# Turning three sets of normalised rows by transposing transfers instead of on the matrix engine, with new order lists

## Chip, cores and metric

The kernel runs on one core of one Trainium2 chip, as one program. The metric is device time in microseconds (us), lower is better. The engines are PE (TensorE, with its weight loads PEld), DVE (VectorE), ACT (ScalarE), POOL (GpSimd) and SP (SyncE, which issues every transfer of this kernel).

## What is computed

The input is `x` of shape (2, 4096, 512) in f32. Two blocks follow each other, each with a residual:

```python
x = x + time_mix(layernorm(x))      # k = x@Wk.T, r = v = x@Wr.T, RWKV recurrence, sigmoid(r)*y, @Wo
x = x + ffn(layernorm(x))
def ffn(x):
    h = rmsnorm(x, gamma1)
    q = h @ Wq + bq;  kv = (h @ Wdown + bdown) @ Wup + bup      # latent of 64
    x = x + (softmax_over_heads(q k / sqrt(32)) v) @ Wo + bo    # 16 heads attend to each other per token
    h2 = rmsnorm(x, gamma2)
    gate = softmax(h2 @ Wg + bg)
    return x + einsum('btd,edf,bte->btf', h2, We, gate)         # 8 experts, all dense
```

Every large product is done in three f16 passes: an operand is split into a high and a low half (`x_hi`, `x_lo`), and hi·hi, lo·hi and hi·lo are summed (`PASSES`). So a product needs its activations as two f16 halves with channels on the partitions, while normalisation needs tokens on the partitions. The step between them is a turn, three times per tile: `mix_turn` (input of the time mix), `att_turn` (input of attention) and `fin_turn2` (input of gate and experts).

## The kernel before

The tokens are cut into `NT` = 32 tiles of 256 tokens, two subtiles (`SUB`) of 128, alternating between the two batch rows. Each engine runs a program of its own through `pipeline` (L561): a head list, then a list `X_ORDER` repeated for `i` = 4 to 30, then a tail list. An entry ("moe", 7, 4) means: step `moe` with part 7 for tile i − 4. So the order on every engine is fixed by hand-written lists, several tiles are in flight, and an engine that waits holds up all that stands behind it in its list. The engines meet through semaphores: `Steps` counts them, `done(t, step, k)` gives the value to wait for.

Per tile the steps that matter here are:

- `pre_load` (SP, L636) brings `xk`, `pre_stats` and `pre_norm` make the layernorm rows, `mix_turn` turns them, `mix_k` and `mix_v` (48 matmuls of 256 columns each) project. DVE then scans the recurrence in two halves (`mix_decay`, `mix_sum`, `mix_value`, `mix_scan`, `mix_rec`, `mix_gate`, `mix_split`), and `mix_project` (24 matmuls) multiplies by Wo.
- `att_norm`, `att_turn`, `att_latent`, `att_q`, `att_up` make q, k and v. SP restacks q and k with 24 transfers (`att_up`, L646). `att_max` 0 to 3 computes 8 banks of scores whose row maxima DVE reduces (L1234), `att_m` turns the maxima, which SP sends back as two extra rows of `qs`, `att_scores` and `att_probs` 0 to 7 follow. DVE's `att_vlo` (L1229) makes the low half of v.
- `fin_back`, `fin_project` give `x2`, `fin_square` and `fin_norm2` its rows, `fin_turn2` turns them into `h2t`, `fin_gate` is the gate's product, `moe_gate` its softmax on DVE, and `moe` 0 to 15 are 8 experts times 2 subtiles, 12 matmuls of 512 columns each (L1333), each added to `acc` by DVE (L1311). PE's `moe` u waits for DVE's `moe` u − 2, as there are two banks. `moe_store` (L667) stores `acc`. There is one `h2t`, so its writer waits for the last `moe` of the tile before.

A turn before the change is 8 matmuls against the identity (`turn`, L1349) into two PSUM banks, then per bank one ACT instruction for the high half and one DVE instruction for the low half (`lo`):

```python
ins = nc.tensor.transpose(banks[b][:, c * T + s * P:c * T + (s + 1) * P],
                          rows_[:, s, (2 * b + c) * P:(2 * b + c + 1) * P], ident[:, :])
...
act.wait_ge(*fin_pe.done(t, "T2", b))
nc.scalar.activation(h2t[:, 0, 2 * b:2 * b + 2, :], mix_bank[b][:, :], ACT.Copy, scale=XS)
...
lo(h2t[:, 1, 2 * b:2 * b + 2, :], mix_bank[b][:, :], XS, h2t[:, 0, 2 * b:2 * b + 2, :])
```

The banks are shared: 0 and 1 for the experts, 2 and 3 for the time mix, both output projections, the turns and the gate, 4 to 7 a ring for attention (`ATT_USES`).

## Time and profile before

| | |
|---|---|
| median of 3 runs | 2760.3 us (2759.11 to 2760.59) |
| profiled execution, its own time | 2758.6 us |
| its span | 2756.5 us |
| mean granted PE clock | 0.975 |
| busy share of the span: PE, DVE, ACT, POOL | 94%, 77%, 56%, 34% |
| transfers | 119.29 MB, all but the instructions' own on one queue, issued by SP |

The span goes from the first to the last instruction, and the execution's own time is 2.1 us longer. A busy share is a mean over start-up, steady part and end. A granted clock of 1.00 is 2.4 GHz, 0.50 is 1.2 GHz. In a timeline an entry merges neighbouring instructions of one line, and its length reaches beyond the start of the next entry, since the ends of matmuls are modelled and pipelined; so durations below are taken from start to start.

### The profile page before, as it was taken

How to read it: one execution, taken by the hardware profiler on the slowest of the kernel's cores; microseconds unless marked ns; L12 is line 12 of the kernel's file. 1: busy time of each engine (PE TensorE's matmuls, PEld its weight loads, DVE VectorE, ACT ScalarE, POOL GpSimd, SP SyncE). 2: the span in 40 equal slices, each digit the busy share in tenths (PEclk: the TensorE clock that was granted, in tenths of full speed). 3: DMA queues.
4: the chain of work that ended last, by engine and by line, in shares of the span. 5: the costliest groups of instructions: out<-in, count | busy, mean ns of one | idle time of the engine just before them, and what ended most of it. 6: DMA issues, size and time to landing. Idle time of an engine off the chain costs nothing.

```text
span 2756.5 us, 48625 instructions
## 1 busy us (share of the span) xinstructions
PE 2586.4 (94%) x18896; PEld 1580.4 (57%) x18896; DVE 2133.6 (77%) x3647; ACT 1531.3 (56%) x2799; POOL 948.9 (34%) x970
## 2 busy tenths in 40 slices
...
DMA packets 845322, 119.29 MB, mean 43 GB/s; under 512 B 813587, under 2 KB 813715, under 8 KB 845075
## 3 DMA queue, kind: packets, MB, share of 16 engines
...
## 4 chain that ended last, share of the span: by engine, by line
PE 88%; DVE 4%; ACT 4%; POOL 2%; SPq 1%; issue 1%; DMA 0%; ACTq 0%; DVEq 0%; POOLq 0%
PE bank L1333 78%; PE bank L1355 3%; PE bank L1500 2%; PE bank L1471 2%; PE bank L1511 2%; DVE h2t L1104 1%; PE bank L1487 1%; POOL w_e L693 1%; ACT h2t L939 1%; PE bank L1512 1%; ACT ot L789 1%; DVE mcol L1234 0%; ACT t L888 0%; POOL pr L734 0%; DVE acc L1311 0%
## 5 line engine op out<-in xcount | busy, mean ns | idle before, releaser
L1333 PE MATMUL bank<-w_e,h2t 128*128 128x512 f16 x6144 | 1383.4, 380 | 2.8 <-DVE acc L1311 2.0
L1333 PEld LDWEIGHTS bank<-w_e,h2t 128*128 128x128 f16 x6144 | 592.1, 98 | 665.9 <-issue 4.4
L1311 DVE SCALAR_TENSOR_TENSOR acc<-bank,gates,acc 128x512 f32<-128x512 f32 x512 | 371.9, 736 | 120.4 <-PE bank L1333 117.4
L906 ACT ACTIVATE pr<-bank,plog,col 128x512 f32<-128x512 f32 x256 | 198.7, 776 | 407.9 <-PE bank L1500 405.5
L734 POOL TENSOR_TENSOR pr<-pr 128x512 f16<-128x512 f32 x256 | 295.7, 1160 | 182.3 <-ACT pr L908 180.9
L721 POOL TENSOR_TENSOR qo<-t,qo 128x256 f16<-128x256 f32 x128 | 106.5, 832 | 493.4 <-ACT qo L891 490.3
L1142 DVE TENSOR_TENSOR_SCAN wkv<-e,wkv 128x256 f32<-128x256 f32 x256 | 210.8, 864 | 74.6 <-ACT e L834 73.4
L1166 DVE RECIPROCAL zz<-zz 128x256 f32<-128x256 f32 x128 | 218.9, 1732 | 29.4 <-POOL zz L703 29.3
L1333 PE MATMUL bank<-w_o,xo 128*128 128x512 f16 x768 | 176.2, 387 | 46.9 <-DVE xo L1104 46.9
L908 ACT ACTIVATE pr<-bank,plog,col 128x512 f16<-128x512 f32 x256 | 197.8, 773 | 0.0
L1333 PE MATMUL bank<-xo,w_k 128*128 128x256 f16 x1536 | 172.9, 273 | 2.4 <-DVE xo L1104 2.4
L1333 PE MATMUL bank<-xo,w_r 128*128 128x256 f16 x1536 | 172.9, 273 | 0.5 <-ACT xk L814 0.5
L1333 PE MATMUL bank<-ht,w_q 128*128 128x256 f16 x1536 | 173.2, 273 | 0.0
L1333 PE MATMUL bank<-w_o,oo 128*128 128x512 f16 x768 | 171.0, 379 | 1.0 <-DVE oo L1104 1.0
L750 POOL TENSOR_TENSOR acc<-x,x 128x512 f32<-128x512 f32 x64 | 80.3, 1276 | 261.5 <-DMA result<-acc 261.5
L1333 PEld LDWEIGHTS bank<-xo,w_k 128*128 128x128 f16 x1536 | 150.0, 98 | 26.0 <-DVE xo L1104 2.7
L1234 DVE TENSOR_REDUCE mcol<-bank 128x4 f32<-128x512 f32 x256 | 158.3, 681 | 3.6 <-PE bank L1487 3.6
L1249 DVE TENSOR_REDUCE on<-bank 128x132 f32<-128x264 f32 x256 | 103.3, 424 | 74.3 <-PE bank L1512 74.3
L1333 PEld LDWEIGHTS bank<-ht,w_q 128*128 128x128 f16 x1536 | 150.5, 98 | 17.5
L1333 PEld LDWEIGHTS bank<-xo,w_r 128*128 128x128 f16 x1536 | 150.2, 98 | 17.8 <-issue 0.8
L1333 PEld LDWEIGHTS bank<-w_o,xo 128*128 128x128 f16 x768 | 75.0, 99 | 134.2 <-DVE xo L1104 47.2
L703 POOL TENSOR_TENSOR zz<-wkv,zz 128x512 f32<-128x512 f32 x64 | 94.1, 1470 | 158.4 <-DVE ev L1153 158.3
...
## 6 DMA issues: line engine op xcount, KB each, us to landing
qs<-qo SPq DMA_DIRECT2D x384, 64.0 KB, 2.4
ks<-k SPq DMA_DIRECT2D x384, 64.0 KB, 2.4
...
ks<-in_attn_Wr SPq DMA_DIRECT2D x1, 1024.0 KB, 10.0
```

The source lines that it names most:

```text
L703: nc.gpsimd.tensor_tensor(zz[:, :, :], wkv[:, 2, :, 0:T], zz[:, :, :], ALU.add).then_inc(mix_pool.sem, 1)
L721: nc.gpsimd.tensor_tensor(grouped(dst, 1)[:, :, b, :], t32[:, b % 2, :].rearrange("p (g j) -> p g j", g=G), grouped(dst, 0)[:, :, b, :], A ...
L734: nc.gpsimd.tensor_tensor(pr16[:, 1, k % 2, :], pr[:, k % 2, :], pr16[:, 0, k % 2, :], ALU.subtract).then_inc(att_pool.sem, 1)
L906: nc.scalar.activation(pr[:, k % 2, :], att_bank[ATT_BANK["S", k]][:, :], ACT.Exp, bias=plog[:, 0:1], scale=colof["soft"])\
L908: nc.scalar.activation(pr16[:, 0, k % 2, :], att_bank[ATT_BANK["S", k]][:, :], ACT.Exp, bias=plog[:, 0:1], scale=colof["soft"])\
L1142: V.tensor_tensor_scan(wkv[:, n, c, 1:T + 1], e1[:, c, :], src[:, c, :], wkv[:, n, c, 0:1], ALU.mult, ALU.add).then_inc(mix_dve.sem, 1)
L1166: V.reciprocal(zz[:, c, :], zz[:, c, :]).then_inc(mix_dve.sem, 1)
L1234: V.tensor_reduce(mcol[:, 4 * k:4 * k + 4], att_bank[ATT_BANK["M", k]][:, :].rearrange("p (g x) -> p g x", g=4), AX, ALU.max).then_inc(att ...
L1249: V.tensor_reduce(on[:, 4 * k:4 * k + 4, :], pv.rearrange("p g (l d) -> p g d l", l=2), AX, ALU.add).then_inc(att_dve.sem, 1)
L1311: V.scalar_tensor_tensor(out=acc[:, s, :], in0=moe_bank[u % 2][:, :], scalar=gates[:, s, e:e + 1], in1=acc[:, s, :], op0=ALU.mult, op1=ALU ...
L1333: ins = nc.tensor.matmul(dst, left(a), right(b), start=(n == 0), stop=(n == last))
L1355: ins = nc.tensor.transpose(banks[b][:, c * T + s * P:c * T + (s + 1) * P], rows_[:, s, (2 * b + c) * P:(2 * b + c + 1) * P], ident[:, :])
```

## The change

The 8 matmuls of each turn go. ACT and DVE now split the rows before they are turned, token by token (two instructions each per turn, as before, now from SBUF to SBUF): high and low halves of 128 x 512 f16 values per subtile, into buffers laid over others (`row16` over `v32`, `hr16` over `k16`, `on16` over `on`). SP then issues four transposing transfers per turn, each of 128 KB, of which each waits for its half of its subtile; they land in `xo16`, `ht16` and `h2t`. PE waits for all four. The writer of `h2t` is now SP, which waits for the last `moe` of the tile before. New waits keep the laid-over buffers apart. The turns' PSUM uses are gone, and the attention ring has two uses fewer. The order lists of all five engines are written anew. The diff, cut (heads, tails and the lists of ACT and POOL are left out but for a few lines; `att_turn` and `fin_turn2` on ACT and DVE change as `mix_turn` does):

```diff
-ATT_USES = ([("T", 0), ("T", 1), ("D", 0), ("Q", 0), ("Q", 1), ("K", 0), ("K", 1), ("V", 0), ("V", 1),
+ATT_USES = ([("D", 0), ("Q", 0), ("Q", 1), ("K", 0), ("K", 1), ("V", 0), ("V", 1),
...
 PE_ORDER = [
...
-    ("att_probs", 6, 3), ("att_probs", 7, 3), ("mix_turn", 0, 1), ("moe", 9, 4), ("mix_k", 0, 1), ("att_turn", 0, 2),
-    ("mix_v", 0, 1), ("att_latent", 0, 2), ("att_q", 0, 2), ("moe", 10, 4), ("att_up", 0, 2), ("moe", 11, 4),
-    ("moe", 12, 4), ("fin_project", 0, 3), ("moe", 13, 4), ("moe", 14, 4), ("moe", 15, 4), ("fin_turn2", 0, 3),
-    ("att_max", 0, 2), ("att_max", 1, 2), ("fin_gate", 0, 3), ("moe", 0, 3), ("att_max", 2, 2), ("att_max", 3, 2),
...
+    ("moe", 8, 4), ("att_probs", 6, 3), ("att_probs", 7, 3), ("moe", 9, 4), ("moe", 10, 4), ("mix_k", 0, 1),
+    ("mix_v", 0, 1), ("att_latent", 0, 2), ("att_q", 0, 2), ("moe", 11, 4), ("att_up", 0, 2), ("fin_project", 0, 3),
+    ("moe", 12, 4), ("moe", 13, 4), ("moe", 14, 4), ("moe", 15, 4), ("att_max", 0, 2), ("att_max", 1, 2),
+    ("att_max", 2, 2), ("att_max", 3, 2), ("moe", 0, 3), ("att_m", 0, 2), ("fin_gate", 0, 3), ("moe", 1, 3),
+    ("moe", 2, 3), ("att_scores", 0, 2), ("att_scores", 1, 2), ("moe", 3, 3), ("moe", 4, 3), ("att_probs", 0, 2),
...
 DVE_HEAD = [
...
-    ("att_max", 0, 0), ("att_max", 1, 0), ("att_max", 2, 0), ("mix_split", 0, 1), ("mix_decay", 1, 1),
-    ("mix_sum", 1, 1), ("att_max", 3, 0), ("att_m", 0, 0), ("mix_value", 1, 1), ("mix_scan", 1, 1), ("mix_rec", 2, 1),
...
+    ("att_max", 2, 0), ("att_max", 3, 0), ("att_m", 0, 0), ("mix_sum", 1, 1), ("mix_value", 1, 1), ("mix_scan", 1, 1),
...
 DVE_ORDER = [
...
-    ("att_vlo", 0, 2), ("fin_project", 0, 3), ("moe", 13, 4), ("mix_decay", 1, 1), ("moe", 14, 4), ("moe", 15, 4),
-    ("fin_turn2", 0, 3), ("att_max", 0, 2),
...
+    ("mix_rec", 1, 1), ("fin_project", 0, 3), ("mix_gate", 0, 1), ("att_vt", 0, 2), ("moe", 12, 4),
+    ("mix_split", 0, 1), ("moe", 13, 4), ("fin_turn2", 0, 3), ("mix_decay", 1, 1), ("moe", 14, 4), ("moe", 15, 4),
+    ("att_vlo", 0, 2), ("att_max", 0, 2), ("att_max", 1, 2), ("att_max", 2, 2), ("mix_sum", 1, 1), ("att_max", 3, 2),
+    ("att_m", 0, 2), ("moe_gate", 0, 3),
...
 SP_HEAD = [
     ("pre_load", 0, 0), ("set_ident", 0, -1), ("set_load", 0, -1), ("set_load", 1, -1), ("set_load", 2, -1),
-    ("set_load", 3, -1), ("set_load", 4, -1), ("set_experts", 0, -1), ("set_experts", 1, -1), ("mix_k", 0, 0),
-    ("set_experts", 2, -1), ("set_experts", 3, -1), ("set_experts", 4, -1), ("set_experts", 5, -1),
-    ("pre_load", 0, 1), ("set_experts", 6, -1), ("set_experts", 7, -1), ("set_masks", 0, -1), ("mix_k", 0, 1),
-    ("att_up", 0, 0), ("att_m", 0, 0), ("pre_load", 0, 2), ("att_up", 0, 1), ("pre_load", 0, 3),
+    ("set_load", 3, -1), ("set_load", 4, -1), ("mix_turn", 0, 0), ("mix_k", 0, 0), ("set_experts", 0, -1),
+    ("set_experts", 1, -1), ("set_experts", 2, -1), ("set_experts", 3, -1), ("set_experts", 4, -1),
+    ("set_experts", 5, -1), ("set_experts", 6, -1), ("set_experts", 7, -1), ("set_masks", 0, -1), ("pre_load", 0, 1),
+    ("mix_turn", 0, 1), ("mix_k", 0, 1), ("att_turn", 0, 0), ("att_up", 0, 0), ("att_m", 0, 0), ("pre_load", 0, 2),
+    ("mix_turn", 0, 2), ("att_turn", 0, 1), ("att_up", 0, 1), ("fin_turn2", 0, 0), ("att_m", 0, 1),
+    ("pre_load", 0, 3), ("mix_k", 0, 2), ("mix_turn", 0, 3), ("att_turn", 0, 2),
 ]
 
 SP_ORDER = [
-    ("mix_k", 0, 2), ("att_m", 0, 3), ("att_up", 0, 2), ("pre_load", 0, 0), ("moe_store", 0, 4),
+    ("att_up", 0, 2), ("fin_turn2", 0, 3), ("moe_store", 0, 4), ("pre_load", 0, 0), ("att_m", 0, 2), ("mix_k", 0, 1),
+    ("mix_turn", 0, 0), ("att_turn", 0, 1),
 ]
 
...
+        row16 = v32[:, :, :].rearrange("p b t -> p (b t)").bitcast(F16).rearrange("p (l s c) -> p l s c", l=2, s=SUB)
...
+        on16 = on[:, :, :].rearrange("p g d -> p (g d)")[:, 0:SUB * C].bitcast(F16).rearrange("p (l s c) -> p l s c", l=2, s=SUB)
...
+        hr16 = k16[:, :, :, :].rearrange("p l b t -> p l (b t)").rearrange("p l (s c) -> p l s c", s=SUB)
...
+        turn_in = Steps(sem("turn_in"), 16, x=4)
+        turn2_in = Steps(sem("turn2_in"), 16, h=4)
+        turn1_in = Steps(sem("turn1_in"), 16, h=4)
...
+            def mix_turn(t, _):
+                if t.back(1):
+                    sp.wait_ge(*mix_pe.done(t.back(1), "O"))
+                for s in range(SUB):
+                    for l, (steps, step) in enumerate(((mix_act, "x_hi"), (mix_dve, "x_lo"))):
+                        sp.wait_ge(*steps.done(t, step, s))
+                        sp.dma_start(xo16[:, l, :, s * P:(s + 1) * P], row16[:, l, s, :], transpose=True).then_inc(turn_in.sem, 16)
...
+            def att_turn(t, _):
+                if t.back(1):
+                    sp.wait_ge(*att_dve.done(t.back(1), "vt"))
+                for s in range(SUB):
+                    for l, (steps, step) in enumerate(((att_act, "h_hi"), (att_dve, "h_lo"))):
+                        sp.wait_ge(*steps.done(t, step, s))
+                        sp.dma_start(ht16[:, l, :, s * P:(s + 1) * P], hr16[:, l, s, :], transpose=True).then_inc(turn1_in.sem, 16)
...
+            def fin_turn2(t, _):
+                if t.back(1):
+                    sp.wait_ge(*moe_pe.done(t.back(1), "u"))
+                else:
+                    sp.wait_ge(elo_done, E * CB)
+                for s in range(SUB):
+                    for l, (steps, step) in enumerate(((fin_act, "h2_hi"), (fin_dve, "h2_lo"))):
+                        sp.wait_ge(*steps.done(t, step, s))
+                        sp.dma_start(h2t[:, l, :, s * P:(s + 1) * P], on16[:, l, s, :], transpose=True).then_inc(turn2_in.sem, 16)
...
             def mix_turn(t, _):
-                for b in range(2):
-                    act.wait_ge(*mix_pe.done(t, "T", b))
-                    if b == 0 and t.back(1):
-                        act.wait_ge(*mix_pe.done(t.back(1), "O"))
-                    nc.scalar.activation(xo16[:, 0, 2 * b:2 * b + 2, :], mix_bank[b][:, :], ACT.Copy, scale=XS)\
-                        .then_inc(mix_act.sem, 1)
+                if t.back(1):
+                    act.wait_ge(*mix_dve.done(t.back(1), "e2v_1"))
+                for s in range(SUB):
+                    act.wait_ge(*pre_act.done(t, "norm", s))
+                    nc.scalar.activation(row16[:, 0, s, :], xk_rows[:, s, :], ACT.Copy, scale=XS).then_inc(mix_act.sem, 1)
...
             def mix_turn(t, _):
-                for b in range(2):
-                    dve.wait_ge(*mix_act.done(t, "x_hi", b))
-                    lo(xo16[:, 1, 2 * b:2 * b + 2, :], mix_bank[b][:, :], XS, xo16[:, 0, 2 * b:2 * b + 2, :]).then_inc(mix_dve.sem, 1)
+                for s in range(SUB):
+                    dve.wait_ge(*mix_act.done(t, "x_hi", s))
+                    lo(row16[:, 1, s, :], xk_rows[:, s, :], XS, row16[:, 0, s, :]).then_inc(mix_dve.sem, 1)
 
...
+                if k == 0 and t.back(1):
+                    dve.wait_ge(*turn2_in.done(t.back(1), "h"))
...
 
-                if use == "T":
+                if use == "K":
                     if t.back(1):
                         pe.wait_ge(*mix_dve.done(t.back(1), "x1", k))
-                elif use == "K":
-                    pe.wait_ge(*mix_dve.done(t, "x_lo", k))
                 elif use == "V":
                     pe.wait_ge(*mix_act.done(t, "k", k))
...
 
-            def mix_turn(t, _):
-                if not t.back(1):
-                    pe.wait_ge(ident_in, 16)
-                pe.wait_ge(*pre_act.done(t, "norm"))
-                turn(xk_rows, mix_bank, mix_pe, mix_pe.sem, lambda b: mix_free(t, "T", b))
-
...
-                pe.wait_ge(*mix_dve.done(t, "x_lo"))
+                pe.wait_ge(*turn_in.done(t, "x"))
...
 
             pipeline(pe, PE_HEAD, PE_ORDER, PE_TAIL,
-                     {f"set_{name}": lambda _, k, name=name: set_turn(name, k) for name in TURNED} | {"mix_turn": mix_turn, "mix_k": mix_k, "mix_v": mix_v, "mix_project": mix_project,
-                          "att_turn": att_turn, "att_latent": att_latent, "att_q": att_q, "att_up": att_up, "att_max": att_max, "att_m": att_m, "att_scores": att_scores, "att_probs": att_probs,
...
```

## Rows read from the trace of the kernel before

**Rows 1.** The page: busy time by engine, with shares of the span.

```profile
PE 2586.4 (94%) x18896; PEld 1580.4 (57%) x18896; DVE 2133.6 (77%) x3647; ACT 1531.3 (56%) x2799; POOL 948.9 (34%) x970
```

**Rows 2.** Busy time by stretch in the steady part (span, PE, PEld, DVE, ACT, POOL, PEclk, DMA).

```profile
1000.00:1500.00 500.00, 495.26 (x3667) 306.21 (x3666) 404.77 (x680) 284.91 (x518) 175.94 (x181) 1.00 0.23 40
```

**Rows 3.** PE over one tile's period (start us, us, line, tile, count, idle before).

```profile
1200.72 5.34 PE L1333 MATMUL bank<-w_e,h2t 128*128 128x512 f16 x24
...
1230.52 1.22 PE L1355 MATMUL bank<-ident,xk 128*128 128x128 f32 x8
1231.57 2.75 PE L1333 MATMUL bank<-w_e,h2t 128*128 128x512 f16 x12
...
1274.53 1.04 PE L1355 MATMUL bank<-ident,ot 128*128 128x128 f32 x8
1275.40 1.06 PE L1487 MATMUL bank<-ks,qs 104*128 104x128 f16 x16
1277.20 0.76 PE L1333 MATMUL bank<-w_g,h2t 128*128 128x8 f16 x24 [0.74 <-DVE h2t L1104]
1277.82 2.75 PE L1333 MATMUL bank<-w_e,h2t 128*128 128x512 f16 x12
1280.41 1.06 PE L1487 MATMUL bank<-ks,qs 104*128 104x128 f16 x16
1281.30 5.34 PE L1333 MATMUL bank<-w_e,h2t 128*128 128x512 f16 x24
```

**Rows 4.** DVE over the same period.

```profile
1265.87 1.22 DVE L1229 TENSOR_TENSOR vp<-hrow,vp 128x1024 f16<-128x1024 f32 x1
...
1274.80 0.75 DVE L1311 SCALAR_TENSOR_TENSOR acc<-bank,gates,acc 128x512 f32<-128x512 f32 x1 [0.82 <-PE bank L1333]
...
1277.06 2.48 DVE L1234 TENSOR_REDUCE mcol<-bank 128x4 f32<-128x512 f32 x4
...
1279.45 0.23 DVE L1285 SCALAR_TENSOR_TENSOR gl<-bank,col,bg_row 128x16 f32<-128x16 f32 x1
...
1282.15 0.75 DVE L1311 SCALAR_TENSOR_TENSOR acc<-bank,gates,acc 128x512 f32<-128x512 f32 x1
...
1285.86 1.39 DVE L1142 TENSOR_TENSOR_SCAN wkv<-e,wkv 128x256 f32<-128x256 f32 x2
```

**Rows 5.** SP's queue over the same period: issues of transfers.

```profile
1254.57 5.64 SPq L655 DMA_DIRECT2D qs<-qo  x8
...
1269.05 2.81 SPq L659 DMA_DIRECT2D ks<-k  x4
```

**Rows 6.** The page: DMA packets, and issues with size and time to landing.

```profile
DMA packets 845322, 119.29 MB, mean 43 GB/s; under 512 B 813587, under 2 KB 813715, under 8 KB 845075
...
qs<-qo SPq DMA_DIRECT2D x384, 64.0 KB, 2.4
```

**Rows 7.** PE busy time and granted clock (PEclk) around one idle stretch late in the run.

```profile
2490.00:2491.00 1.00, 0.00 (x0) 0.88 0.76 91
2491.00:2497.00 6.00, 5.53 (x60) 0.50 0.69 182
2497.00:2498.00 1.00, 1.00 (x5) 0.70 0.00 0
```

**Rows 8.** PE around the same idle stretch.

```profile
2491.47 0.81 PE L1333 MATMUL bank<-w_g,h2t 128*128 128x8 f16 x24 [3.40 <-DVE h2t L1104]
...
2495.70 3.69 PE L1333 MATMUL bank<-w_e,h2t 128*128 128x512 f16 x12
```

**Rows 9.** PE in the start-up.

```profile
23.60 5.40 PE L1333 MATMUL bank<-xo,w_k 128*128 128x256 f16 x48
...
81.79 8.30 PE L1333 MATMUL bank<-w_o,xo 128*128 128x512 f16 x24 [46.88 <-DVE xo L1104]
...
155.64 0.40 PE L1493 MATMUL bank<-ident,mcol 128*32 128x128 f32 x1 [11.22 <-DVE mcol L1234]
```

**Rows 10.** SP's queue in the start-up.

```profile
32.03 0.91 SPq L626 DMA_DIRECT2D bg_row<-in_ffn_bg  x2
```

More of the change, by code:

```diff
@@ L146 @@
-    ("att_probs", 2, 0), ("att_scores", 4, 0), ("att_probs", 3, 0), ("att_scores", 5, 0), ("att_probs", 4, 0),
-    ("att_scores", 6, 0), ("att_probs", 5, 0), ("att_scores", 7, 0), ("mix_project", 0, 1), ("mix_turn", 0, 2),
-    ("att_probs", 6, 0), ("att_probs", 7, 0), ("mix_k", 0, 2), ("att_turn", 0, 1), ("mix_v", 0, 2),
-    ("att_latent", 0, 1), ("att_q", 0, 1), ("fin_project", 0, 0), ("att_up", 0, 1), ("fin_turn2", 0, 0),
-    ("fin_gate", 0, 0), ("att_max", 0, 1), ("att_max", 1, 1), ("att_max", 2, 1), ("moe", 0, 0), ("att_max", 3, 1),
@@ L154 @@
+    ("att_latent", 0, 1), ("att_q", 0, 1), ("fin_project", 0, 0), ("att_up", 0, 1), ("att_max", 0, 1),
+    ("att_max", 1, 1), ("att_max", 2, 1), ("att_max", 3, 1), ("moe", 0, 0), ("att_m", 0, 1), ("fin_gate", 0, 0),
+    ("moe", 1, 0), ("moe", 2, 0), ("att_scores", 0, 1), ("att_scores", 1, 1), ("moe", 3, 0), ("moe", 4, 0),
+    ("att_probs", 0, 1),
 ]
 PE_ORDER = [
-    ("att_scores", 4, 3), ("moe", 7, 4), ("att_probs", 3, 3), ("att_scores", 5, 3), ("moe", 8, 4),
-    ("att_probs", 4, 3), ("att_scores", 6, 3), ("att_probs", 5, 3), ("att_scores", 7, 3), ("mix_project", 0, 2),
@@ L170 @@
-    ("att_probs", 4, 4), ("att_scores", 6, 4), ("att_probs", 5, 4), ("att_scores", 7, 4), ("mix_project", 0, 3),
-    ("moe", 9, 5), ("mix_turn", 0, 2), ("att_probs", 6, 4), ("att_probs", 7, 4), ("moe", 10, 5), ("mix_k", 0, 2),
-    ("mix_v", 0, 2), ("att_turn", 0, 3), ("fin_project", 0, 4), ("att_latent", 0, 3), ("att_q", 0, 3),
-    ("att_up", 0, 3), ("moe", 11, 5), ("moe", 12, 5), ("moe", 13, 5), ("fin_turn2", 0, 4), ("moe", 14, 5),
-    ("moe", 15, 5), ("fin_gate", 0, 4), ("att_max", 0, 3), ("att_max", 1, 3), ("att_max", 2, 3), ("att_max", 3, 3),
@@ L180 @@
-    ("att_probs", 7, 3), ("mix_k", 0, 1), ("mix_v", 0, 1), ("att_turn", 0, 2), ("moe", 10, 4), ("moe", 11, 4),
-    ("att_latent", 0, 2), ("att_q", 0, 2), ("att_up", 0, 2), ("fin_project", 0, 3), ("moe", 12, 4), ("moe", 13, 4),
-    ("moe", 14, 4), ("moe", 15, 4), ("fin_turn2", 0, 3), ("fin_gate", 0, 3), ("att_max", 0, 2), ("att_max", 1, 2),
-    ("att_max", 2, 2), ("att_max", 3, 2), ("moe", 0, 3), ("att_m", 0, 2), ("moe", 1, 3), ("moe", 2, 3),
-    ("att_scores", 0, 2), ("att_scores", 1, 2), ("moe", 3, 3), ("att_probs", 0, 2), ("att_scores", 2, 2),
```

412 lines of the change are left out of this document (206 added, 206 removed), and 3 rows, old and new, of the table POOL_HEAD.

## The prediction

> **What bounds the kernel now.** I read the page's busy times first: PE is busy for 94% of the span, DVE for 77% [rows 1]. A share over the whole run hides the stages, so I went on to stretches: in the steady part PE is busy for 495.3 of 500 us at full clock, DVE for 404.8 [rows 2]. So PE's own work sets the pace there, and what it stops doing is worth its full length, if nothing else becomes late. PE's timeline gives the period of a tile: the same pair of expert steps starts at 1200.72 and 1281.30, 80.58 us apart [rows 3].
>
> **What the change takes from PE.** The time mix's turn takes 1231.57 - 1230.52 = 1.05 us, the experts' turn 1275.40 - 1274.53 = 0.87 [rows 3]; attention's stands between them in form and count and I take 0.87 too. That is 2.79 us per tile, 89 us in 32 tiles. PE also waits 0.74 us per tile for the halves of `h2t` before the gate [rows 3]. If nothing else moved, 3.5 us per tile would go: over the 29 tiles of the sum below 102 us, or 2657. ACT and DVE keep two instructions each per turn, of the same size and count, now from SBUF. I cost that at nothing: both have idle time in a period, DVE 19% of it [rows 2]. The PSUM uses that go free banks that nobody was seen to wait for.
>
> **What it puts in their place.** I follow each turn in the new lists.
>
> *Experts.* This is the place that decides. There is one `h2t`, so SP may begin its four transfers only when `moe` 15 of the tile before is done, and `moe` 0 needs all four. Between them PE now has only `att_max` 0 to 3; then come `moe` 0, `att_m`, `fin_gate`, `moe` 1, `moe` 2. Call the end of `moe` 15 time 0. Before, `moe` 2 started at 1281.30 + 2.59 - 1274.53 = 9.4 (a `moe` step is 1280.41 - 1277.82 = 2.59) [rows 3]. The rest of the period is 80.6 - 9.4 = 71.2; without the two other turns, and with `att_m` (0.1) moved into the stretch, it becomes 69.2. The new period is 69.2 plus the new start of `moe` 2.
>
> Even with free transfers DVE's list sets a floor for it. DVE reads `moe` 15 from 0.27 for 0.67 us, then does `att_vlo` (1.14 of its 1.22, as neighbours overlap by 0.08), six reductions of 0.60, `mix_sum` (1.3) and two more reductions: 8.2 us [rows 4]. Before, `att_vlo` was long done and `mix_sum` came later; now both lie ahead of `att_m`, which on PE lies ahead of the gate. After `att_m` the gate's product takes 0.6 [rows 3], and from the first instruction of `moe_gate` to the end of `moe` 0 on DVE are 1282.15 + 0.67 - 1279.45 = 3.4 us [rows 4], for which `moe` 2 waits: 8.2 + 0.1 + 0.6 + 0.2 + 3.4 = 12.5. The period would be 81.7, **1.1 us longer than now**, although PE has 2.8 us less to do.
>
> Now the transfers. No row shows a transposing one. The nearest is SP's restacking: a 64 KB transfer occupies SP's queue for 5.64 / 8 = 0.70 us [rows 5] and lands 2.4 us after its issue began [rows 6], 1.7 after its end. With 384 for q and as many for k, and 813,587 packets under 512 B, a transfer is some 1,060 pieces of 64 bytes [rows 6]. A turn's transfer has twice the bytes. I take twice the time, **1.4 us each**, on the guess that the cost goes with the pieces; the ends are 0.70 (it costs what the row shows) and 2.8 (its pieces are half as long). The last of four lands at 0.1 + 5.6 + 1.7 = 7.4 (4.6 at the low end, 13.0 at the high). `moe` 0 then runs from 7.4 to 10.0, `att_m` and gate end at 10.7, and 0.2 + 3.4 later `moe` 2 starts, at 14.2: +2.8 us per tile. At the low end the floor of 12.5 stands; a landing up to 5.6 costs nothing.
>
> The Trainium skill (Advanced Engine Details and Errata, DMA Advanced Topics, on the X-bar transpose) says that transposing transfers run as fast as plain ones. By that the sum would end at its low end, near 2783.
>
> *The clock.* Between 0 and 7.4 PE has 1.8 us of work. Late in the run PE stood idle for 3.4 us before a gate [rows 8]; by the shares of two rows its clock fell to 0.50, which is 1.2 GHz, at 2490.8 and came back at 2497.6 [rows 7], and the `moe` step in between is listed with 3.69 us [rows 8] instead of 2.75 [rows 3]. The new stretch holds over 5 us of idleness in 7.4, so I expect this in every tile: of some 6.8 us at half clock about 4 fall on `moe` 0 and the gate's product, and half of those are lost: +2.0. Per tile **+4.8 us**.
>
> *Time mix.* From the end of `mix_project` to `mix_k` PE has three `moe` steps and four short ones, about 8.6 us. DVE still has the second update of `x1` and the first low half to make, 0.7 each, the size of its `moe` steps [rows 4]; three transfers follow: 1.5 + 4.2 + 1.7 = 7.4. Hidden, and exposed from some 1.8 us per transfer on. *Attention.* It has the two projections more as cover: 96 matmuls of 256 columns, the columns of four `moe` steps, 10.4 us. Hidden as well.
>
> *SP.* Twelve transfers more are 16.8 us of its queue per tile, beside 24 x 0.70 = 16.9 for restacking and a few loads, within 80. `fin_turn2` stands behind `att_up`, whose last issue ended at 1269.05 + 2.81 = 1271.86 [rows 5]. PE's way from `att_q` to `att_max` becomes one `moe` step and one turn shorter, 3.46 us, so on that tile's scale `moe` 15 would end at 1275.40 - 3.46 = 1271.94: SP is free just then, and the last of `ks` lands 1.6 us later, which the floor hides. Behind `fin_turn2` wait `moe_store`, `pre_load` and `att_m`'s two transfers; the last is needed after 11, SP is free at 7.
>
> *Start-up.* SP reaches the first turn only after the constants, at 33 us [rows 10]; with 5.6 + 1.7 `mix_k` starts at 40, not at 23.6 [rows 9]. But PE then waited 46.9 us for `mix_project` [rows 9] on DVE and ACT work for weights that the new lists put later; I make it 2 us later in all. Against that, `att_m` waited 11.2 us because `mix_sum` stood ahead of it on DVE [rows 9], and no longer does. Net -8 (+15 to -25).
>
> *Sum.* 27 periods and two more in head and tail: 29 x 4.8 = +139, -8. The profiled execution took 2758.6 us (1.7 below the median of 2760.3): **2890 us**.
>
> **Rivals.**
>
> - *Cheap transfers, or the clock holds.* Landing below 5.6, or no fall: +1.1 to +2.8 per tile, 2783 to 2832. For it: the restacking rows. Against: the idleness.
> - *Dearer transfers.* At 2.8 us each `moe` 0 starts at 13.0, and with more of it at half clock `moe` 2 at 22.3: +10.9 per tile, 3067. Should a piece be 8 bytes (5.6 us each), `moe` 0 starts at 24 and the time mix's turn shows by 15 us as well: +38 per tile, about 3850. The Trainium skill (VectorE: DVE Perf Modes, the three transpose paths) gives 1309 ns for one 128x128 block by transposing DMA; four blocks in a row would be 5.2 us, and with that this worst case. DMA is only 23% busy [rows 2], which speaks against it.
> - *Faster.* The turns pay in full, 29 x 3.5: 2657. Place: between `moe` 15 and `moe` 2. It needs `moe` 2 to start by 11.4, where the 2.8 us saved balance; DVE's list gives 12.5 at the least, so it needs reductions or the gate's softmax 1.1 us shorter and transfers landed by 4.5.
> - *No change*: the low end, with a start-up some 25 us shorter.
>
> **Chances.** Forecast 0.50 (2835 to 2960), cheap 0.20, dearer 0.15, worst 0.04, faster 0.07, no change 0.04. A measurement here can tell about 0.2%, 5.5 us. The range, 2783 to 3060, spans the two ends of a transfer's price.
>
> **What would show it.** In the new profile: L1355 gone from PE; between `moe` 15 and `moe` 0 an idle stretch ended by a transfer into `h2t`, about 5 us per tile; granted clock below 1.00 once per tile; a period near 85.4; transposing issues of 1.4 us on SP; `mix_k` and `att_latent` without waits. I am wrong if `moe` 2 starts within 11 us of `moe` 15's end, or if the period is below 80.6.

## The result, and the profile after

The changed kernel takes 2887.94 us (median of 3 runs, 2886.72 to 2896.34) against 2760.3, a ratio of 1.0475 with a 95% interval of 1.0459 to 1.0491. It is slower, as forecast (2890, range 2783 to 3060). The profiled execution took 2896.3 us with a span of 2894.2, so it stands 8.4 us above the median; the one of before stood 1.7 below its own.

The page of after, busy times [rows 1] and the chain that ended last:

```profile
PE 2607.8 (90%) x18128; PEld 1529.4 (53%) x18128; DVE 2096.8 (72%) x3647; ACT 1527.1 (53%) x2799; POOL 963.8 (33%) x970
...
PE 66%; SPq 14%; ACT 8%; DVE 4%; DMA 3%; POOL 3%; issue 2%; ACTq 0%; DVEq 0%; POOLq 0%
```

The chain of before:

```profile
PE 88%; DVE 4%; ACT 4%; POOL 2%; SPq 1%; issue 1%; DMA 0%; ACTq 0%; DVEq 0%; POOLq 0%
```

PE has 768 instructions less (24 per tile, the turns) and is busy *longer*. What it no longer does is made up elsewhere: the expert products, unchanged in number, are listed with 1443.5 us instead of 1383.4, mostly because of `moe` 0 at half clock (below), and those of `att_max` with 103.7 instead of 73.9. SP's queue now holds 14% of the chain, where it held 1%.

The last wait of each stage is seen best in PE's waits by what ended them, for the stretch 500 to 2500 us (some 24 tiles; us in total, times, longest):

```profile
PE bank L1501 <- DMA ks<-k: 47.8, 23, 3.3
PE bank L1361 <- DMA h2t<-on: 29.6, 23, 2.9
PE bank L1501 <- DVE mcol L1261: 10.1, 39, 0.7
```

Before, the only one of note was that for the halves of `h2t`:

```profile
PE bank L1333 <- DVE h2t L1104: 21.2, 25, 3.4
```

In the changed kernel there is none for the time mix's or attention's transfers. Where does the time go within a tile? PE's timeline between `moe` 15 and `moe` 2, first in one of the 3 of 27 steady tiles in which `moe` 0 ran at full clock [rows 3 has the stretch of before]:

```profile
1255.80 3.67 PE L1501 MATMUL bank<-ks,qs 104*128 104x128 f16 x32 [2.19 <-DMA ks<-k]
1260.55 2.76 PE L1361 MATMUL bank<-w_e,h2t 128*128 128x512 f16 x12 [1.08 <-DMA h2t<-on]
1263.15 0.27 PE L1507 MATMUL bank<-ident,mcol 128*32 128x128 f32 x1
...
1263.87 2.75 PE L1361 MATMUL bank<-w_e,h2t 128*128 128x512 f16 x12
1267.09 2.76 PE L1361 MATMUL bank<-w_e,h2t 128*128 128x512 f16 x12 [0.47 <-DVE acc L1339]
```

and one tile on, as in most:

```profile
1338.63 1.58 PE L1501 MATMUL bank<-ks,qs 104*128 104x128 f16 x20 [2.18 <-DMA ks<-k]
...
1343.33 5.12 PE L1361 MATMUL bank<-w_e,h2t 128*128 128x512 f16 x12 [1.11 <-DMA h2t<-on]
1348.28 0.27 PE L1507 MATMUL bank<-ident,mcol 128*32 128x128 f32 x1
...
1349.00 5.56 PE L1361 MATMUL bank<-w_e,h2t 128*128 128x512 f16 x24
```

`moe` 15 ends at 1255.80 - 2.19 = 1253.61 and 1338.63 - 2.18 = 1336.45, and `moe` 0 starts 6.9 us later in both. In the first, `moe` 2 starts 13.5 us after `moe` 15's end, in the second 1349.00 + 2.6 - 1336.45 = 15.2; before it was 9.4. The rest of the period is 82.84 - 13.5 = 69.4 us. The second tile's `moe` 0 takes 5.1 us instead of 2.8, with the same shape, count and operands. The granted clock (third column from the end) shows why, and shows that it fell in the first tile too, only earlier:

```profile
1256.00:1259.00 3.00, 3.00 (x30) 2.63 (x28) 2.68 (x5) 0.29 (x1) 0.00 (x0) 0.50 0.40 88
1343.00:1348.00 5.00, 4.67 (x12) 1.64 (x13) 2.23 (x4) 0.00 (x0) 2.48 (x2) 0.50 0.62 210
```

In the first tile PE ran at 0.50 during `att_max` and was back at full clock before `moe` 0. It lost next to nothing by that: `att_max` took 3.67 us, and in the second tile, where the clock fell only behind 1341, 1341.61 + 0.61 - 1338.63 = 3.6, with waits for DVE's reductions in between. The two other tiles with a fast `moe` 0 show the same (0.50 from 1680 to 1682 and from 2103 to 2105 us). So the clock falls in every steady tile, and in 24 of 27 the fall lies on `moe` 0. SP's queue and DVE in the second tile [rows 5, rows 4]:

```profile
1290.71 5.20 SPq L654 DMA_TRANSPOSE xo<-v  x4
1300.61 5.12 SPq L667 DMA_TRANSPOSE ht<-k  x4
1318.93 5.65 SPq L678 DMA_DIRECT2D qs<-qo  x8
...
1333.98 2.82 SPq L682 DMA_DIRECT2D ks<-k  x4
1336.90 5.23 SPq L698 DMA_TRANSPOSE h2t<-on  x4
```

```profile
1339.07 3.68 DVE L1261 TENSOR_REDUCE mcol<-bank 128x4 f32<-128x512 f32 x6 [0.33 <-PE bank L1501]
1342.66 1.38 DVE L1170 TENSOR_TENSOR_SCAN wkv<-e,wkv 128x256 f32<-128x256 f32 x2
1343.97 1.26 DVE L1261 TENSOR_REDUCE mcol<-bank 128x4 f32<-128x512 f32 x2
1348.60 0.28 DVE L1267 TENSOR_SCALAR m<-bank 32x128 f16<-32x128 f32 x1 [3.37 <-PE bank L1507]
```

A transposing transfer holds SP for 1.3 us, and the last of four lands 1343.33 - 1342.13 = 1.2 us after its issue ended. SP is busy with hardly a gap from 1318.93 to 1342.13: restacking, then the experts' turn. DVE is done with the maxima at 1345.2 and then waits 3.4 us for `att_m`, which stands behind the slow `moe` 0 on PE. DVE isn't the bound here.

A tile's period is read from the start of `att_m`'s one matmul, one row for 32 tiles; here of after, then of before (ns min/median/max, first and last start):

```profile
L1507 PE MATMUL bank<-ident,mcol x32: 272/273/421, 154.0 to 2789.5; 128*32 128x128 f32 x32
```

```profile
L1493 PE MATMUL bank<-ident,mcol x32: 272/273/396, 155.6 to 2663.3; 128*32 128x128 f32 x32
```

From tile 2 to tile 25 the mean period is 84.71 us after and 80.61 before: **+4.10**. Of the 137.7 us between the two spans, 94.3 lie in these 23 periods, 12.7 in the start-up (`att_m` of tile 2 at 331.7 instead of 318.9) and 30.6 in the last six tiles and the end. The profile of after stands 8.4 us above its median, some 0.3 us per tile, so its periods are a little long against the medians.

### The profile page after: what moved, and what is told of

Its sections match the earlier page's. It is cut to its first block, busy times and chain, and to the rows that moved or that the text cites. A ratio compares the mean times of both kernels' runs of the same rounds, so it can differ in the third digit from the quotient of the medians.

```text
span 2894.2 us, 47472 instructions
## 1 busy us (share of the span) xinstructions
PE 2607.8 (90%) x18128; PEld 1529.4 (53%) x18128; DVE 2096.8 (72%) x3647; ACT 1527.1 (53%) x2799; POOL 963.8 (33%) x970
## 4 chain that ended last, share of the span: by engine, by line
PE 66%; SPq 14%; ACT 8%; DVE 4%; DMA 3%; POOL 3%; issue 2%; ACTq 0%; DVEq 0%; POOLq 0%
PE bank L1361 61%; SPq L678 5%; SPq L698 4%; SPq L682 4%; DMA h2t<-on 3%; PE bank L1514 2%; ACT t L921 2%; PE bank L1525 1%; ACT qo L924 1%; PE bank L1485 1%; ACT e L862 1%; ACT e L858 1%; POOL w_e L726 1%; PE bank L1526 1%; DVE acc L1339 1%
## 5 line engine op out<-in xcount | busy, mean ns | idle before, releaser
L1361 PE MATMUL bank<-w_e,h2t 128*128 128x512 f16 x6144 | 1443.5, 392 | 51.5 <-DMA h2t<-on 45.5
L1361 PEld LDWEIGHTS bank<-w_e,h2t 128*128 128x128 f16 x6144 | 600.3, 100 | 777.9 <-issue 77.4
L767 POOL TENSOR_TENSOR pr<-pr 128x512 f16<-128x512 f32 x256 | 317.2, 1244 | 298.9 <-ACT pr L941 276.2
L1170 DVE TENSOR_TENSOR_SCAN wkv<-e,wkv 128x256 f32<-128x256 f32 x256 | 236.0, 963 | 103.7 <-ACT e L866 102.4
L1194 DVE RECIPROCAL zz<-zz 128x256 f32<-128x256 f32 x128 | 219.1, 1733 | 13.5 <-POOL zz L736 13.5
L1501 PE MATMUL bank<-ks,qs 104*128 104x128 f16 x1024 | 103.7, 262 | 111.7 <-DMA ks<-k 93.0
L1361 PE MATMUL bank<-xo,w_k 128*128 128x256 f16 x1536 | 179.2, 278 | 25.5 <-DMA xo<-v 25.5
L972 ACT ACTIVATE gl<-gl 128x16 f32<-128x16 f32 x32 | 6.9, 215 | 339.9 <-DVE gl L1319 339.9
```

What stands on the lines that cost most here:

```text
L767: nc.gpsimd.tensor_tensor(pr16[:, 1, k % 2, :], pr[:, k % 2, :], pr16[:, 0, k % 2, :], ALU.subtract).then_inc(att_pool.sem, 1)
L1170: V.tensor_tensor_scan(wkv[:, n, c, 1:T + 1], e1[:, c, :], src[:, c, :], wkv[:, n, c, 0:1], ALU.mult, ALU.add).then_inc(mix_dve.sem, 1)
L1194: V.reciprocal(zz[:, c, :], zz[:, c, :]).then_inc(mix_dve.sem, 1)
L1361: ins = nc.tensor.matmul(dst, left(a), right(b), start=(n == 0), stop=(n == last))
```

## Experiments

Three theories were set against each other. *Landing*: the loss sits between `moe` 15 and `moe` 2, since SP may write `h2t` only after `moe` 15. *Clock*: half of it is PE's clock falling in that gap. The rivals: SP's full queue (late `ks`), DVE's list, or the two hidden turns. All ratios below are to the kernel before, run on the same chip.

### The clock: spare products in the gap

```diff
+            def spare(t, count):
+                pe.wait_ge(*fin_dve.done(t, "x2", 1))
+                for _ in range(count):
+                    nc.tensor.matmul(mix_bank[1][:, :], w16["e0"][:, 0, 0, 0:P], w16["e0"][:, 0, 0, :], start=True, stop=True)
```

called with 8 ahead of `att_max` 0 and with 4 ahead of `moe` 0.

> The changed kernel with spare products in PE's two gaps (results thrown away): 8 matmuls of 512 columns between moe 15 and att_max 0, 4 between att_max 3 and moe 0, 0.22 us each, so 1.7 and 0.9 us inside gaps of 2.2 and 1.1 us. Clock theory: moe 0 runs for 5.0 us where the granted clock is 0.50 and 2.6 us where it is 1.00; kept busy, PE keeps its clock, the period goes from 84.7 to 82.6 us and the run from 2888 to about 2825. Rival, the clock falls for another reason or the loss is only the transfers': 2888, or a little more.

Measured: 2854.5 us, ratio 1.0348 (1.0333 to 1.0364), period 83.20. Busy times and granted clock (third column from the end) over 500 to 2500 us, then PE in one tile:

```profile
500.00:2500.00 2000.00, 1941.52 (x13873) 1139.38 (x13872) 1545.13 (x2646) 1089.61 (x1973) 696.47 (x700) 1.00 0.32 58
```

```profile
1399.18 1.89 PE L1496 MATMUL bank<-w_e 128*128 128x512 f16 x8
...
1406.33 2.76 PE L1361 MATMUL bank<-w_e,h2t 128*128 128x512 f16 x12 [1.00 <-DMA h2t<-on]
...
1412.90 2.76 PE L1361 MATMUL bank<-w_e,h2t 128*128 128x512 f16 x12 [0.50 <-DVE acc L1339]
```

In the changed kernel the clock of the same window was 0.96, and 24 of 27 tiles lost 2.2 us each at `moe` 0. With PE kept busy `moe` 0 runs at full clock in nearly every tile, though it still waits for its rows. That is worth 33 us by the medians, and 1.5 of the 4.1 us per tile by the profiles; the other 2.6 stay. I had expected 2.1 per tile and 2825 us. Part of what is missing is that PE now waits for DVE at `moe` 2, here 0.5 us and 10.4 us in all between 500 and 2500.

### SP's queue: four restacking transfers less

```diff
                         for n in first:
+                            if name == "k" and n == 2 and t.back(1):
+                                continue
```

> The changed kernel without 4 of the 24 restacking transfers of each tile but the first (rows 64 to 95 of ks keep the first tile's values, so attention's scores are others). SP is then free 2.8 us earlier and ks lands 2.8 us earlier. Landing theory (h2t's transfers can't start before moe 15 is done, whatever SP does): only the 0.4 us between moe 15's end and SP's first issue goes, and the 2.2 us wait of att_max turns into a longer wait of moe 0: 2888 - 31 x 0.4 = about 2875. Rival, SP's queue or DVE's reductions after the late ks set the end: 2.2 to 2.8 us less per tile, 2801 to 2820.

Measured: 2878.8 us, ratio 1.0434 (1.0418 to 1.0449): 9 us less than the changed kernel, period 84.17. In one tile of it:

```profile
1414.15 5.14 SPq L701 DMA_TRANSPOSE h2t<-on  x4
```

```profile
1413.95 1.06 PE L1504 MATMUL bank<-ks,qs 104*128 104x128 f16 x16
1417.05 0.40 PE L1504 MATMUL bank<-ks,qs 104*128 104x128 f16 x4 [2.04 <-DVE mcol L1264]
...
1420.49 5.15 PE L1364 MATMUL bank<-w_e,h2t 128*128 128x512 f16 x12 [1.03 <-DMA h2t<-on]
```

`att_max` starts at once, its wait goes elsewhere in the stretch, and `moe` 0 still starts 1420.49 - 1413.95 = 6.5 us after `moe` 15. So the largest wait in the list of waits, 47.8 us for `ks`, is worth 9: what ends the stretch is the landing of `h2t`. The theory that SP's late `ks` sets the pace, worth 2.2 to 2.8 us per tile, falls.

### The price of the landing: half the transfers, and twice as many

```diff
                         sp.wait_ge(*steps.done(t, step, s))
+                        if l == 1 and t.back(1):
+                            continue
                         sp.dma_start(h2t[:, l, :, s * P:(s + 1) * P], on16[:, l, s, :], transpose=True).then_inc(turn2_in.sem, 16)
```

> The changed kernel with only the two high halves of the experts' rows turned (the low halves in h2t keep the first tile's values). SP's part falls from 5.2 to 2.6 us. Landing theory: moe 0 no longer waits for a transfer and starts when att_max 3 is done, 1.1 us earlier: 2888 - 31 x 1.1 = 2854 if the clock falls as before, 2790 if it holds in every tile. Rival, DVE's list (att_vlo, reductions, mix_sum) holds att_m and with it moe 2: no gain beyond 0.5 us per tile, 2872 or more.

```diff
                         sp.dma_start(h2t[:, l, :, s * P:(s + 1) * P], on16[:, l, s, :], transpose=True).then_inc(turn2_in.sem, 16)
+                for n in range(2 * SUB):
+                    sp.dma_start(ot[:, :].bitcast(F16).rearrange("p (n b t) -> p n b t", n=4, b=CB)[:, n, :, :], on16[:, n % 2, n // 2, :], transpose=True).then_inc(turn2_in.sem, 16)
```

> The changed kernel with four more transposing transfers behind the experts' own four (same rows, into a buffer that is free then); moe 0 and the gate wait for all eight. Landing theory: SP's part grows from 5.2 to 10.4 us, moe 0 starts 5.2 us later and runs at half clock in every tile: +5.2 to +6 us per tile, 3050 to 3075. Rival, the price of a transfer is mostly the fixed wait for its landing, or DVE's list holds the stretch: +2.6 us per tile or less, under 2970.

Measured: half 2844.5 us, 1.0309 (1.0294 to 1.0324), period 82.91, -1.8; twice 3051.5 us, 1.1061 (1.1045 to 1.1078), period 89.71, +5.0. Four more transfers cost their 5.2 us of SP in full, as the landing theory has it; two fewer give back less than 2.6 (1.8, with the clock still falling), so that another bound shows below. PE's wait in the second kernel:

```profile
PE bank L1363 <- DMA ot<-on: 150.9, 23, 7.8
```

### The bound below: DVE's list

In `h2_half` PE waited for the maxima at `att_m` in 11 tiles. To keep the clock out of it, a pair was run with the 8 spare products, without and with this change of DVE's list:

```diff
-("moe", 14, 4), ("moe", 15, 4), ("att_vlo", 0, 2), ("att_max", 0, 2), ("att_max", 1, 2), ("att_max", 2, 2), ("mix_sum", 1, 1), ("att_max", 3, 2),
+("att_vlo", 0, 2), ("moe", 14, 4), ("moe", 15, 4), ("att_max", 0, 2), ("att_max", 1, 2), ("att_max", 2, 2), ("att_max", 3, 2),
...
-("moe", 0, 4), ("moe", 1, 4), ("mix_value", 1, 2),
+("moe", 0, 4), ("moe", 1, 4), ("mix_sum", 1, 2), ("mix_value", 1, 2),
```

> h2_half (only the high halves of the experts' rows turned) with 8 spare products in PE's wait between moe 15 and att_max 0, so that the clock holds. Floor theory: att_m waits for DVE's list (att_vlo, reductions, mix_sum), which ends 7.6 us after att_max began whatever the clock; moe 2 starts 13.1 us after moe 15 as in h2_half, the period is that of the tiles of h2_half in which the clock held, 82.3 us, and the run 2820 to 2844. Rival (DVE is no bound, only the clock): the period falls below 81.5 us, under 2805.

> h2_half_fill with DVE's list changed as in h2_half_dve (att_vlo ahead of moe 14, mix_sum's second half behind moe 1). Floor theory: with the clock held, att_m no longer waits for DVE and moe 2 starts 1.2 us earlier, 31 x 1.2 = 37 us less than h2_half_fill, less 1.0 us per tile if att_probs waits for POOL as in h2_half_dve: a difference of -6 to -37 us. Rival: as slow against h2_half_fill as h2_half_dve was against h2_half, +24 us; then the moved steps cost more elsewhere than DVE's list costs there.

Measured: 2854.5 (1.0345, 1.0329 to 1.0360) and 2836.3 us (1.0284, 1.0267 to 1.0301), periods 83.43 and 82.50. The first, by PE, DVE and POOL:

```profile
1410.82 2.76 PE L1364 MATMUL bank<-w_e,h2t 128*128 128x512 f16 x12
1415.22 0.28 PE L1517 MATMUL bank<-ident,mcol 128*32 128x128 f32 x1 [1.65 <-DVE mcol L1264]
...
1415.95 7.03 PE L1364 MATMUL bank<-w_e,h2t 128*128 128x512 f16 x24
```

```profile
1411.64 2.35 DVE L1173 TENSOR_TENSOR_SCAN wkv<-e,wkv 128x256 f32<-128x256 f32 x2
```

```profile
1411.81 3.23 POOL L786 TENSOR_TENSOR acc<-x,x 128x512 f32<-128x512 f32 x2 [14.00 <-DMA result<-acc]
```

Here the floor of the prediction is seen: PE stands 1.65 us for DVE's maxima, and the clock, kept at `moe` 0, falls one step later (`moe` 1 and 2 take 7.03 us, not 5.56). Such a 7.03 us pair stands in 8 of the steady tiles, and in others `moe` 0 is slow all the same. So the first run missed both of its forecasts: the 8 spare products, which should have kept the clock, made `h2_half` 10 us slower. The mean granted clock was 0.957, against 0.951 without them.

Moving the two DVE steps away is worth 18 us, within what was expected. PE's waits in the second run, 500 to 2500 us:

```profile
PE bank L1534 <- POOL pr L769: 23.4, 49, 0.7
PE bank L1510 <- DVE mcol L1263: 15.8, 76, 0.3
PE bank L1510 <- DMA ks<-k: 13.4, 17, 1.6
```

With half the transfers, a clock that mostly holds and DVE's list eased, the period is still 82.50, 1.9 us above that of before. What is left are these waits, of which that for POOL came with the moved steps, and the 1.7 us of spare products. So half of the landing, the clock and DVE's list together give back 2.2 of the 4.1 us, and what the rest would take isn't isolated.

The same change of DVE's list without spare products made the kernel slower:

> h2_half (only the high halves of the experts' rows turned, the low ones in h2t keep the first tile's values) with DVE's list changed: att_vlo ahead of moe 14, and mix_sum's second half behind moe 1 instead of between the reductions. Floor theory: in h2_half att_m waits for DVE, whose list between moe 15 and att_m is 2.5 us longer than it need be; without that moe 2 starts 1.5 us earlier, 2844 - 31 x 1.5 = 2798. Rival, DVE is no bound there: 2844 unchanged, or slower for what the moved steps now hold up.

Measured: 2868.2 us (1.0381, 1.0358 to 1.0403), 24 more than `h2_half`. The period grew by 1.2 us, from 82.91 to 84.08. The list of PE's waits has one that `h2_half` didn't have, 1.0 us per tile:

```profile
PE bank L1527 <- POOL pr L769: 23.0, 48, 0.5
```

And `moe` 0 took 5.2 us in one tile, at 1419.48, and 3.9 in the corresponding one of `h2_half`; the mean clock was 0.944 against 0.951. How the 24 us divide between POOL and the clock is not shown.

### The time mix's turn: how well is it hidden?

The same addition to `mix_turn`, from `row16` into the dead `xk`.

> The changed kernel with four more transposing transfers behind the time mix's own four (into the rows' old buffer); mix_k waits for all eight. In the changed kernel the last one lands 2.3 us before mix_k starts. So 5.2 us more should show as 2.9 us per tile: 2888 + 31 x 2.9 = 2978. With the slack of the prediction, 1.2 us, it would be +4.0, 3012. Rival, a wait at mix_k only takes the place of the waits for ks and h2t later in the tile (SP's queue gains the same time): less than 1 us per tile, under 2920.

Measured: 3047.7 us, 1.1043 (1.1026 to 1.1059), period 89.19, +4.5. PE's waits, and `mix_k` itself:

```profile
PE bank L1363 <- DMA xk<-v: 70.5, 22, 3.8
```

```profile
1372.76 7.08 PE L1363 MATMUL bank<-xo,w_k 128*128 128x256 f16 x48 [3.70 <-DMA xk<-v]
```

The wait is 3.2 us per tile, so 5.2 us more leave 2.0 hidden: the slack, nearly as the profile of after had it. But in most tiles part of `mix_k` then also runs at half clock, and it is listed with 7.08 us, not the 5.4 of the changed kernel. I had left that out, and 2978 was too low by 70. A wait of some 3 us on PE costs 4.5 to 5.

### Is the experts' turn alone to blame?

The obvious repair leaves the experts' turn on PE (code of before) and the two others to transfers. It was tried with three sets of steady lists, DVE's following PE's. PE's, first:

```diff
-("moe", 15, 4), ("att_max", 0, 2), ("att_max", 1, 2), ("att_max", 2, 2), ("att_max", 3, 2), ("moe", 0, 3), ("att_m", 0, 2), ("fin_gate", 0, 3), ("moe", 1, 3), ("moe", 2, 3), ("att_scores", 0, 2), ("att_scores", 1, 2), ("moe", 3, 3), ("moe", 4, 3), ("att_probs", 0, 2),
+("moe", 15, 4), ("fin_turn2", 0, 3), ("att_max", 0, 2), ("att_max", 1, 2), ("fin_gate", 0, 3), ("moe", 0, 3), ("att_max", 2, 2), ("att_max", 3, 2), ("moe", 1, 3), ("moe", 2, 3), ("att_m", 0, 2), ("moe", 3, 3), ("moe", 4, 3), ("att_scores", 0, 2), ("att_scores", 1, 2), ("moe", 5, 3), ("att_probs", 0, 2),
```

> The turn of the time mix and that of attention by transfers as in the changed kernel, the experts' turn on PE as before, with the order between moe 15 and moe 3 as before. Landing theory (all of the loss sits at h2t, the two other turns are hidden): PE keeps 1.9 us less to do than before, the period is 78.7 to 79.5 us, the run 2700 to 2730, faster than both. Rival, the two hidden turns cost too (their transfers, or the longer chain through SP's queue): a period of 80.6 us or more, 2760 and above.

The second, from `att_scores` 5 to `moe` 11:

```diff
+("att_scores", 5, 3), ("mix_project", 0, 2), ("att_probs", 4, 3), ("att_scores", 6, 3), ("att_probs", 5, 3), ("att_scores", 7, 3), ("moe", 8, 4), ("att_probs", 6, 3), ("att_probs", 7, 3), ("moe", 9, 4), ("mix_k", 0, 1), ("mix_v", 0, 1), ("att_latent", 0, 2), ("att_q", 0, 2), ("moe", 10, 4), ("att_up", 0, 2), ("moe", 11, 4),
```

> As experts_pe (time mix's and attention's turn by transfers, the experts' on PE), with the steady lists rewoven to take out its two waits, 2.8 us per tile of att_probs for POOL and 1.4 us of att_max for ks: moe 8 steps stand between the scores as before, mix_project stands one step earlier, and moe 10 stands behind att_q and no longer ahead of mix_k. If the transfers of these two turns are hidden wherever the lists leave them cover, the period falls from 83.4 to 79 us and the run to 2720, faster than before. Rival: there isn't enough other work on PE for both covers, the 8 us that the time mix's transfers need after mix_project and the 22 us that the restacking needs after att_q; then what one wait loses another gains, and the run stays above 2760.

The third, the same stretch:

```diff
+("att_scores", 5, 3), ("moe", 8, 4), ("att_probs", 4, 3), ("att_scores", 6, 3), ("mix_project", 0, 2), ("att_probs", 5, 3), ("att_scores", 7, 3), ("att_probs", 6, 3), ("moe", 9, 4), ("att_probs", 7, 3), ("moe", 10, 4), ("mix_k", 0, 1), ("mix_v", 0, 1), ("att_latent", 0, 2), ("att_q", 0, 2), ("moe", 11, 4), ("att_up", 0, 2),
```

> As experts_pe2, with moe 8 ahead of att_probs 4, mix_project one step later and moe 10 back ahead of mix_k. That should end the two waits of att_probs for POOL (1.7 us per tile) and that of mix_project for DVE (1.4), and cost 1.4 us at ks again, since 20.8 us of PE work then stand between att_q and att_max and the restacking needs 22.2. Cover theory (PE's other work in a tile isn't enough to cover the time mix's transfers and the restacking and the time mix's own chain on DVE, so each list only moves the wait): 82.9 - 1.7 = 81.2 us per tile, 2849 - 27 x 1.7 = about 2800, still not faster than before. Rival (the lists of experts_pe2 were only unlucky): 79 us per tile and under 2755.

Measured: 2863.1 (1.0376, 1.0358 to 1.0393), 2849.0 (1.0328, 1.0313 to 1.0344) and 2839.8 us (1.0293, 1.0278 to 1.0309); periods 83.52, 83.22, 82.82. The waits of PE in 500 to 2500 us, for the first, the second and the third:

```profile
PE bank L1521 <- POOL pr L757: 66.2, 70, 1.6
PE bank L1497 <- DMA ks<-k: 33.4, 24, 2.8
```

```profile
PE bank L1521 <- POOL pr L757: 39.7, 48, 0.9
PE bank L1355 <- DVE xo L1127: 33.5, 24, 1.4
```

```profile
PE bank L1497 <- DMA ks<-k: 36.9, 24, 2.3
PE bank L1521 <- POOL pr L757: 35.6, 50, 1.3
PE bank L1355 <- DMA xo<-v: 13.1, 24, 1.3
```

My landing theory had forecast 2700 to 2730 here, and that fell; the third run, too, came out 40 us above what I had expected. Each set of lists ends one wait and opens another. PE's `moe` steps are the cover for everything that takes time elsewhere: 6.7 us for the time mix's rows after `mix_project` (0.2 to the first issue, 5.2 for the four, 1.3 to the landing), 22 us for the restacking after `att_q`, POOL's 8 low halves between the scores. A turn by transfers needs such cover, and may take it from another step where no wait for its own rows is seen. That this is what happens is argued, not shown: in these kernels the transfers and the lists changed together, and the time mix's turn was not moved alone in the lists of before. Better lists may exist; none of the three was faster than before.

### Attention's turn alone

The kernel before, with the changed kernel's `att_turn` on SP, ACT and DVE, none on PE, and the lists of before but for (steady part; head and tail of SP and the tail of ACT likewise):

```diff
 ACT_ORDER
-("att_norm", 0, 3), ("mix_k", 0, 2), ("fin_back", 0, 4), ("att_turn", 0, 3),
+("att_norm", 0, 3), ("att_turn", 0, 3), ("mix_k", 0, 2), ("fin_back", 0, 4),
 DVE_ORDER
-("mix_turn", 0, 1), ("att_stats", 0, 2), ("att_norm", 0, 2), ("fin_back", 0, 3), ("att_turn", 0, 2),
+("att_stats", 0, 2), ("mix_turn", 0, 1), ("att_norm", 0, 2), ("att_turn", 0, 2), ("fin_back", 0, 3),
 SP_ORDER
-("mix_k", 0, 2), ("att_m", 0, 3), ("att_up", 0, 2),
+("mix_k", 0, 2), ("att_m", 0, 3), ("att_turn", 0, 2), ("att_up", 0, 2),
```

> The kernel before with attention's turn alone by transfers, in the lists of before but for these moves: att_stats ahead of the time mix's low halves and att_turn ahead of fin_back on DVE, att_turn right behind att_norm on ACT, on SP ahead of att_up. PE has 0.87 us less per tile. From the end of mix_project to att_latent PE has 14.5 us of other work (att_probs, the time mix's turn, moe 9, mix_k, mix_v); the rows need about 6.1 us to the first issue (second update of x1, statistics, norm, high half), the four issues 5.2 and the landing 1.2: 12.5 us. Theory (a turn by transfers pays where PE has its whole latency as cover and SP is idle): no new wait, 31 x 0.87 = 27 us less, 2733, faster than before. Rival (attention's turn isn't hidden either, since in the changed kernel the same rows took 16.3 us from mix_project to the last landing): 1.8 us of waiting for a gain of 0.87, and the clock may fall: 2787 or more.

Measured: 2769.8 us, ratio 1.0039 (1.0025 to 1.0053). Steady part of this kernel:

```profile
PE bank L1345 <- DVE xo L1117: 9.0, 24, 0.4
PE bank L1345 <- DMA ht<-k: 2.6, 1, 2.6
```

The transfers are hidden in every steady tile (the one wait for `ht` is near the end of the window, where the tail begins), and the period is 80.28, 0.3 us *less* than before; 0.4 of the 0.87 went to a new wait of `mix_k` for DVE, behind the statistics that I had moved ahead of it. But the run is 10 us longer: `att_m` of tile 2 comes 5.3 us later (10.2 us of waiting for `ht` in the start-up), and from tile 25's `att_m` to the end it takes 596.7 us instead of 583.6, 8.7 of them in three waits for `ht`; DVE's list of the end was left as it was. So one of the three turns does pay in the steady part, and loses more in start-up and end. No version beat the kernel before.

## Why the prediction was right, point by point

- **Sign and size.** 2890 forecast, 2888 measured. The nearness is partly luck: +4.8 per tile was 0.7 more than the 4.1 measured (29 x 0.7 = 20 us), and start-up and end, for which I had -8, came out at 137.7 - 29 x 4.10 = +19 in the profiled execution, which also stands 8 us above the median. The two misses nearly cancel.
- **The place.** As forecast, between `moe` 15 and `moe` 2: rest of the period 69.2 forecast, 69.4 measured. `h2_twice` shows that what SP does there is paid in full.
- **The transfer.** 1.4 us of SP forecast, 1.3 measured; landing 1.7 us after the issue's end forecast, 1.2 measured. `moe` 0 was to start at 7.4 and starts at 6.9: issue and landing are shorter than forecast, although SP begins 0.45 us after `moe` 15, not 0.1. The number came out right, but not the reason. I had guessed that the cost goes with the pieces, and that there are twice as many as in a restacking transfer. The page of after has:

```profile
DMA packets 1054215, 169.60 MB, mean 59 GB/s; under 512 B 1022482, under 2 KB 1022610, under 8 KB 1053970
```

That is 208,893 packets and 50.31 MB more than before, for 384 transposing transfers: 544 packets of 241 bytes on the mean in each, half as many as the 1,060 of a restacking transfer, and the transfer holds SP's queue for nearly twice as long. The time goes with the bytes here (128 KB in 1.3 us, 64 KB in 0.7); whether that is more than a coincidence of two sizes was not tried. The Trainium skill (Advanced Engine Details and Errata, DMA Advanced Topics, on the X-bar transpose) says that transposing transfers are as fast as plain ones. The trace agrees byte for byte with the restacking, and from the issue's begin to the landing both take about 2.4 us. It doesn't agree for plain transfers in larger pieces: the store of `acc`, 512 KB, holds SP's queue for 0.58 us (from 1342.17 on).
- **The clock.** It was to fall in every tile and cost 2.0 us. It did fall in every tile, in 24 of 27 at `moe` 0, where it cost 2.2 us, 2.0 on the mean; taking the idleness away gave 1.5 back (`fill`). In the tile above in which it fell during `att_max` the period is 82.8, 2.2 more than before, where I had 2.8 without the clock.
- **The DVE floor.** It exists (`h2_half_fill`: 1.65 us) and lies under the landing, as forecast, but higher than I had it: with half the transfers and a fast `moe` 0, `moe` 2 starts 13.0 us after `moe` 15 (`h2_half`, the tile whose `moe` 15 ends at 1565.10), not 12.5, so that only 0.5 us lie between it and the 13.5 of the best tile.
- **`ks` lands late, and that is hidden.** Right: 2.2 us of waiting, worth 9 us of run (`ks_less`).
- **Time mix and attention hidden.** Right in that neither is waited for in the steady part. The time mix's slack was 2.0 to 2.3 us, not 1.2: the first issue came 0.2 us after `mix_project`, not 1.5, since the rows were ready and only `xo16` was not yet free, and all four transfers followed it. Whether the two turns are also hidden at no cost stays open: attention's turn alone cost nothing in the steady part (`att_only`), while in the three `experts_pe` kernels, with both turns moved and new lists, PE waited elsewhere.
- **ACT's and DVE's splitting, put at nothing.** Right as far as busy time shows: it is 4 and 37 us less than before.
- **Start-up and end.** The term that was wrong in sign: -8 us forecast, 12.7 later measured at `att_m` of tile 2. The end, which the prediction had left out, adds 30.6 - 6 x 4.1 = 6 to the steady rate. `att_m` of tile 0 did come 1.6 us earlier, as the 11.2 us wait [rows 9] went, but the next period took 92.6 us instead of 82.7, with 23.5 us of `att_probs` waiting for POOL and 14.2 of `att_max` waiting for `ks`. At the end the last tile's `moe` 0 waits 6.4 us for its rows, where the gate waited 1.6.
- **Rivals.** "Faster" needed `moe` 2 within 11.4 us; it is 13.5 at best. "Dearer" needed 2.8 us per transfer. Its worst case was mis-added: by its own scaling, 5.6 us per transfer belongs to pieces of 16 bytes, and 8 bytes would give 11.2; and with 5.6 the time mix's turn would show by 1.5 + 16.8 + 1.7 - 8.6 = 11, not 15. Nothing else rests on it.
